# An attention and FP4 block on one core: a static order in which GpSimd's jobs and VectorE's SBUF jobs exclude each other

## What is computed

```python
h = _layernorm(x) * (1 + ca) + sa
x = x + ga * attn(h)      # 16 heads of 16, causal, slopes on the position, softmax
h = _layernorm(x) * (1 + cb) + sb
x = x + gb * ffn(h)
# ffn: each product has both sides rounded in blocks of 16 to 8 magnitudes
#   scale = max(|block|) / 6 ; q = nearest grid value(x / scale) * scale
#   gate = q(h) @ q(w_gate).T ; y = q(h) @ q(w_up).T      (256 -> 704)
#   return q(silu(gate) * y) @ q(w_down).T                (704 -> 256)
```

## Time and profile before

| what | value |
|---|---|
| median of 3 runs | 4124.66 us (4122.55 to 4128.27) |
| the profiled execution | 4125.13 us |
| its span, first to last instruction | 4123.1 us |
| TensorE busy | 3656.7 us |
| VectorE busy | 3191.6 us |
| ScalarE busy | 1916.1 us |
| GpSimd busy | 1289.3 us |
| granted clock of TensorE, mean | 0.956 |

### The profile page before, as it was taken

One profiled execution on the slowest core, in us unless ns is written; L12 is line 12 of the kernel. 1 busy time (PEld: TensorE's weight loads), 2 busy tenths in 40 slices (PEclk: granted clock), 3 DMA queues, 4 the chain that ended last, 5 costly groups with the idle time before them and its releaser, 6 DMA issues.

```text
span 4123.1 us, 57870 instructions
## 1 busy us (share of the span) xinstructions
PE 3656.7 (89%) x21300; PEld 1920.1 (47%) x21300; DVE 3191.6 (77%) x6061; ACT 1916.1 (46%) x3471; POOL 1289.3 (31%) x918
## 2 busy tenths in 40 slices
PE   4899989999888989988899899998988999899966
PEld 2344444544444444454544445444454544445435
DVE  9877877787787778878787777877778788776835
ACT  2454544445444544545455454444545455454531
POOL 5214233242332424224142332423224132331223
PEclk7899999999999999999999999999999999999987
DMA  7141322323232331323323332331313313322010
GB/s 130 27 87 28 63 45 50 58 45 60 43 55 40 63 54 31 63 39 56 58 36 54 51 53 49 54 57 37 63 32 63 58 31 59 50 48 44 22 26 11
DMA packets 158188, 205.51 MB, mean 50 GB/s; under 512 B 44036, under 2 KB 98004, under 8 KB 157908
## 3 DMA queue, kind: packets, MB, share of 16 engines
q1 hardware_dynamic: 157908, 201.82, 28.8%
HBM read 63.78 MB, written 17.89 MB: 20 GB/s over the span
## 4 chain that ended last, share of the span: by engine, by line
PE 52%; DVE 27%; DMA 6%; issue 5%; ACT 4%; POOL 4%; SPq 3%; DVEq 0%; POOLq 0%; ACTq 0%
PE banks L681 8%; PE banks L814 8%; PE banks L704 7%; PE banks L664 7%; PE banks L798 6%; DVE banks L1094 5%; PE banks L791 5%; ACT arena L865 3%; DMA xa<-in_x 3%; PE banks L760 3%; PE banks L807 2%; SPq L552 2%; DMA sums<-oT 2%; PE banks L772 2%; PE banks L729 2%
## 5 line engine op out<-in xcount | busy, mean ns | idle before, releaser
L865 ACT ACTIVATE arena<-banks 128x512 f32<-128x512 f32 (+1 forms) x2432 | 1291.4, 582 | 1175.8 <-PE banks L667 748.5
L1094 DVE CUSTOM_DVE_ANT_0 banks<-banks,mask 128x640 f32<-128x640 f32 (+3 forms) x1024 | 1032.6, 1042 | 65.3 <-PE banks L704 58.1
L664 PE MATMUL banks<-qa,ka 105*128 105x512 bf16 (+3 forms) x3072 | 833.9, 332 | 95.7 <-ACT arena L865 70.8
L704 PE MATMUL banks<-ka,qa 102*128 102x512 bf16 (+3 forms) x3072 | 762.8, 335 | 124.7 <-DVE top L1094 87.4
L681 PE MATMUL banks<-arena,va 128*17 128x512 f32 (+3 forms) x6144 | 648.9, 497 | 20.5 <-ACT arena L865 16.4
L664 PEld LDWEIGHTS banks<-qa,ka 105*128 105x128 bf16 x3072 | 281.0, 98 | 657.0 <-ACT arena L865 370.9
L704 PEld LDWEIGHTS banks<-ka,qa 102*128 102x128 bf16 x3072 | 258.7, 99 | 466.6 <-DVE top L1094 162.1
L999 POOL TENSOR_TENSOR hid<-hid,tm 128x704 f32<-128x704 f32 x128 | 217.3, 1698 | 714.2 <-DVE hid L1068 714.2
L1092 DVE TENSOR_REDUCE top<-banks 128x2 f32<-128x768 f32 (+3 forms) x384 | 381.2, 1039 | 57.0 <-PE banks L709 55.4
L814 PE MATMUL banks<-wdT,hqT 128*128 128x256 f32 x1536 | 371.4, 393 | 2.9 <-ACT hqT L908 2.8
L791 PE MATMUL banks<-wguT,xqT 128*128 128x352 f32 x1024 | 333.7, 472 | 0.7 <-ACT xqT L899 0.7
(11 more groups left out here) (146 smaller groups left out, 4894.1 us busy)
## 6 DMA issues: line engine op xcount, KB each, us to landing
qa<-parts SPq DMA_DIRECT2D x384, 128.0 KB, 4.5
ka<-parts SPq DMA_DIRECT2D x384, 128.0 KB, 5.2
xa<-in_x SPq DMA_DIRECT2D x16, 1024.0 KB, 10.0
rsumT<-rsum_dram SPq DMA_DIRECT2D x64, 256.0 KB
onT<-oT SPq DMA_DIRECT2D x256, 64.0 KB, 4.3
xr<-in_x SPq DMA_DIRECT2D x64, 256.0 KB, 2.7
out_x<-xr SPq DMA_DIRECT2D x64, 256.0 KB, 6.3
ffn_rows<-rows_dram SPq DMA_DIRECT2D x16, 384.0 KB, 7.7
```

The source lines that it names most:

```text
L664: mm = pe.matmul(ps[:, m * w:(m + 1) * w], ka[g][0:KT, h, kt * P:(kt + 1) * P], qa[g][0:KT, h, q0:q0 + w], start=heads < G, stop=heads == ...
L704: mm = pe.matmul(ps[:, at:at + z - a], qa[g][0:KS, h0 + m, qt * P:(qt + 1) * P], ka[g][0:KS, h0 + m, a:z], start=qt > 0, stop=qt == 0 or h ...
L865: nc.scalar.activation(probs[:, s % P_SLOTS, j * heads:(j + 1) * heads, 0:w], ps[:, 0:heads * w].rearrange("p (h q) -> p h q", h=heads), A ...
L1094: nc.vector.tensor_tensor_reduce(out=ps, in0=ps, in1=mask[:, S - w:S], scale=1.0, scalar=MASKED, op0=ALU.add, op1=ALU.max, accum_out=tops) ...
```

## The change

`settle()` gets one more rule. It keeps the time at which the last job of GpSimd, and the last job of VectorE whose name is in the list `APART`, ends. A GpSimd job is not planned to start before that VectorE job has ended, and a VectorE job of the list not before GpSimd's has. Two lags grow: XA from 7 to 12 us, MUL from 0.06 (the default) to 8 us. No instruction is added or removed, and no semaphore; the lists come out in another order.

```diff
+    APART = ("LN", "XR", "XQ", "HR", "HQ", "N3", "SM", "WQ", "QROW")
...
+        memory = {"DVE": 0.0, "POOL": 0.0}
...
                 t, where = max(start, earliest[key]), None
+                if key[0] == "POOL":
+                    t = max(t, memory["DVE"])
+                elif key[0] == "DVE" and key[1][0] in self.APART:
+                    t = max(t, memory["POOL"])
...
             self.order[engine].append(event)
+            if engine == "POOL" or engine == "DVE" and event[0] in self.APART:
+                memory[engine] = free[engine]
...
-            p.add("SP", ("XA", b), 0.7, at, ("POOL", ("SPL", b - 1, 3)), lag=7.0)
+            p.add("SP", ("XA", b), 0.7, at, ("POOL", ("SPL", b - 1, 3)), lag=12.0)
...
-            p.add("POOL", ("MUL", b, g // 2), 2.4, due + 10.0, *((("SP", (k, b, n)) for n in (g - 1, g) for k in ("NUM", "RBC"))))
+            p.add("POOL", ("MUL", b, g // 2), 2.4, due + 10.0, *((("SP", (k, b, n)) for n in (g - 1, g) for k in ("NUM", "RBC"))), lag=8.0)
```

## The result

The kernel before took 4123.6 us in the median of these runs (4117.4 to 4128.3), the kernel after 3888.2 us (3883.8 to 3890.9): a ratio of 0.9429, 95% interval 0.9413 to 0.9445.

A forecast was written before the change was run, and what follows sets the result against it. TensorE's own work was taken as the floor, so only its idle time and lower clock could be won. 85.8 + 28 + 53 + 6 - 15 = 158 us off 4125 gave 3967 us, likeliest 3935 to 3995, full range 3895 to 4050.

The forecast's parts named there:

- O's waits: TensorE's waits for MUL before the output projection go, covered by other work, except the last batch's 19.1 us: 85.8 us.
- low clock at O: TensorE's lower clock after the wait at the output projection goes too: 2.0 us by 14 batches, 28 us.
- the two repeated waits: TensorE's waits for VectorE's maxima before score tiles S(b+1,2,17) and S(b+2,0,1): 59 us, of which 60% was taken.
- the clock behind them: Slow clock after those two score-tile waits: 1.3 us by 23 waits, 30 us, of which 60% was taken.
- the start: Three weight quantisations WQ move from before the first score tiles into the first attention stage: gain 0 to 11, taken 6 us.
- what comes back: New loss from transposes T waiting on ScalarE in front of O and from bunched VectorE jobs: 15 us, between 0 and 30.
- XA: Longer lag moves N1 later, so VectorE's 4.29 us stand there is covered; its idle time itself worth nothing.
- Bounds are 0 and 89; I take 60%, 53 us: Gain from planning GpSimd's and VectorE's jobs apart: repeated score-tile waits plus the slow clock behind them.
- Keeping it apart returns nothing: Separating VectorE's reductions in XR and HR from GpSimd only bunches VectorE's jobs, priced at 0 to 1 us a batch.
- L1182's mean under 0.8 us: Sign of success: VectorE's line in LN, 1097 ns in the mean before, is held less by GpSimd.
- rival 3: GpSimd late at HT(.,4), so TensorE waits there 13 times, 69 us; with rival 1, 4095 us; chance 10%.
- rival 4: Slower: split SPL(b+2,0) ahead of XQ(b,0) on GpSimd delays XT and gates; up to 4299 us; chance 5%.

The follow-up runs named there:

- e7: Kernel before, own order, with 24 matmuls more per batch that nothing reads, run while TensorE waits at O: 4095.0 us, ratio 0.9931.
- e5: Kernel after with XA's lag back at 7 us: 3894.5 us, ratio 0.9445.
- e13: Kernel after with XR alone taken out of the list APART: 3892.7 us, ratio 0.9431.
- e11: Kernel after with HR alone taken out of the list APART: 3978.0 us, ratio 0.9644.
- e12: Kernel after with the plan's costs of LN, SM, XQ, HR and HQ set nearer to their undisturbed times: 3935.7 us, ratio 0.9552.
- e15: Kernel after with lags of 10.5 us for XA and 6 us for MUL: 3954.2 us, ratio 0.9585.
- e8: Kernel after with XR and HR both taken out of the list APART: 3984.0 us, ratio 0.9661.

## Why the prediction was wrong, point by point

The direction held, and so did the mechanisms of the parts but for one: that a meeting of the two engines which comes back costs TensorE a wait again. The sum was 77 us short. Against the change of the span, 241.7 us:

| step of the prediction | forecast | measured | from |
|---|---|---|---|
| O's waits | 85.8 | 85.7 | 104.9 to 19.2 |
| low clock at O | 28 | 34.4 busy, 28 in the time | 150.5 to 116.1; e7 |
| the two repeated waits | 35 (60% of 59) | 68.8, all waits for maxima | 87.4 to 18.6 |
| the clock behind them | 18 (60% of 30) | 51.9, all that is not O's; about 43 by the low stretches | 86.3 less 34.4; 46.2 to 3.4 |
| the start | 6 | 15.1, of it 7.2 the wait for WQ | 549.2 to 534.1; 29.3 to 22.1 |
| what comes back | -15 | -29.4, T for ScalarE | 70.8 to 100.2 |
| XA | 0 | 0 to 6 | e5 |

**The step that failed** is "Bounds are 0 and 89; I take 60%, 53 us". All of it came, and more: 68.8 us of waits and 51.9 of busy time, 121 in all. That alone is 68 us, most of the 77. It had two mistakes. The factor of 60% stood for meetings that drift and come back elsewhere. They did come back, in every batch: in after HQ meets the split, as shown. The prediction took a meeting that comes back for a wait that comes back. Behind these meetings no wait of TensorE is over 0.70 us, where it was 2.60 before; it had DN in hand. The other mistake is the price. The clock behind a wait was put at 1.3 us for 23 waits, since "for 4 us work runs at about half speed while part of it waits anyway". Before had 23 low stretches away from O, and TensorE was busy for 92.5 of their 99.0 us, so hardly any part of it waited: 2.0 us each by the half, not 1.3. The window of the earlier trace rows behind such a wait had it already, 4.00 us busy out of 4.00 at 0.57. Six of the 23 lasted longer than the 4 us. At O the price was not argued but read off the matmuls' durations, and it held (e7).

**A statement that was wrong:** "Keeping it apart returns nothing", of the reductions. It is true of their own duration (882 and 884 ns) and of XR (e13, 4 us); but taking HR from the list costs 90 us (e11). I had asked what a job's own time gains from being kept apart, and not what its entry does to the rest of the order: with it DN stands beside the held HQ, without it DN is over before HQ, and TensorE waits 2.18 us in 13 batches (e11). How HR's entry brings DN there was not followed in the plan. The Trainium skill ("SBUF — State Buffer", Who interferes with whom) says that a tensor_reduce does not contend with GpSimd, and that tensor_scalar can, in the modes that take both ports. The traces agree on both: 882 and 884 ns for the reduction, 2.33 us against a median of 527 ns for the TENSOR_SCALAR of HQ. The rule was right and my use of it too narrow.

**What was right:** O's waits to a tenth of a us, with the last one left at 19.2; the low clock at O; L1182's mean under 0.8 us (0.487); no wait at N1; no new wait at HT or XT (25.0 us at HT, 30.3 before; 12.7 at XT in both), so rival 3 did not come, and no split was late, so rival 4 did not. The middle batches came at 231.6 us, below the 237 to 240 that I had named, with the clock at 1.00, above the 0.98.

**What was too small:** "what comes back". T's waits for ScalarE alone grew by 29.4 us, 2.1 us a batch by (100.2 - 70.8) / 14, twice the 15 us that I gave to them and the bunching together. They cost little clock: of all these pieces, none over 1.8 us, one has a low stretch behind it.

**The rest.** The table's measured terms, with the start at 7.2 and 5.3 us that the wait at HT lost, add up to a gain of 223.9 us; 17.8 us of the span are spread over waits that I did not follow.

**What stays open.** What decides whether the clock falls at a short wait: in e11 the same wait of 1.41 us has a low stretch behind it in some batches and none in others, and in after one of 2.15 us has none. At the score tiles the clock's share is an estimate from the low stretches (about 43 us); no run takes it away by itself, as e7 did at O. And why this order, of the ten with the rule (3888 to 4029 us), leaves TensorE with work in hand at the meetings, where e11 does not, is shown at one place and not explained as a rule: small changes of the plan (e12, e15) lost 47 and 66 us.

## What to carry to other kernels

Count a short, repeated wait of TensorE with the clock behind it: here 155 us of idle time saved came with another 86 us of busy time, so read the mean clock of a window and TensorE's busy time for the same matmuls before sizing a change of order. When jobs of two engines are planned apart and some still meet, look at what the engine that bounds the kernel has in hand during the meeting: held for 2.5 us beside DN, VectorE cost TensorE 0.43 us, and held for 3.3 us without it, 2.18 us and the clock behind. The moved job's own duration tells nothing of that. A static order that rests on a cost table is sensitive: try each number of it on the chip, one at a time, since e12's and e15's small changes cost 47 and 66 us.

## What the runs showed of the hardware

- Short waits can bring the clock down, but their length alone does not decide it. Waits of 2.18 and 2.60 us had a clock of 0.58 and 0.57 behind them (e11), and one of 1.41 us had 0.58 (e11); one of 1.00 and one of 2.15 us left it at 1.00 (after). By the mean clock, TensorE was at its lower level for about 2 x (1 - 0.956) x 4123.1 = 363 us in before and 2 x (1 - 0.980) x 3881.4 = 155 us in after; half of the difference is 104 us. Counting only the part of the low time in which TensorE was busy (247.1 and 88.2 us), half is 79.5 us. 86.3 us of busy time were saved. Of e8 against after the same half is 82 us, and 80.7 were measured. The Trainium skill ("TensorE: Matmul & The Clock Gate", HAM oscillation) describes such a swing, at waits for transfers, and counts half of the time at the lower level as lost; these runs agree with the half where TensorE is busy in the low time, and show it at waits of 1.4 to 2.6 us for another engine.
- A TENSOR_SCALAR on 704 fp32 columns of SBUF, 527 ns in the median of its line, took 2.33 us beside a GpSimd TENSOR_TENSOR of 2.28 us (e11), and a TENSOR_TENSOR 2.69 us (0.89 us undisturbed) beside one of 2.27 us (after). Both were held for 1.80 us, and 1.95 and 1.94 us of GpSimd's instruction were left when they started: VectorE stands until the other instruction is nearly over.
- The job that waits for the read of the reciprocal sums (256 KB into 64 partitions) started 7.9 and 8.05 us after its issue, before and after: that did not change with the order. Other transfers were on the queue beside it, so this is not the time of the read alone.
